# Attention shares once per block for all heads, and convolution rows as one 512-column matmul in passes two to four

## What is computed

```python
# attention, for each head h (e is es[src] + ed[dst] after a leaky ReLU)
ex    = exp(e_h - m[dst])
den   = segment_sum(ex, dst)
alpha = ex / maximum(den[dst], 1e-16)
out   = segment_sum(alpha[:, None] * z_h[src], dst)          # added to x

# convolution, used twice, with a PReLU behind each
xt  = x @ W
m   = segment_sum(xt[src], dst) * Binv[:, None]              # Binv = 1/degree, 0 without edges
out = segment_sum(m[dst], src) * Dinv[:, None] + b
```

## Time and profile before

| | us |
|---|---|
| median of 3 runs (2114.61 to 2118.65) | 2115.71 |
| the profiled execution, its own time | 2117.84 |
| the span of that execution, first to last instruction | 2115.9 |
| attention phase, first matmul to the first after it in the experts phase | 478.90 to 1005.95 |
| convolutions, first matmul to the first of the feed-forward | 1243.88 to 1918.49 |

### The profile page before, as it was taken

How to read it: one execution, slowest core, us unless ns; L and a number is a source line. 1 busy time by engine, 2 the same in 40 slices (tenths; PEclk the granted TensorE clock), 3 DMA queues, 4 the chain that set the end, 5 groups by cost and what they waited for, 6 DMA issues and landing times. The chain is left out here.

```text
span 2115.9 us, 42215 instructions
## 1 busy us (share of the span) xinstructions
PE 1749.2 (83%) x13965; PEld 1581.7 (75%) x13965; DVE 1278.1 (60%) x2275; ACT 1139.2 (54%) x1914; POOL 100.7 (5%) x124
## 2 busy tenths in 40 slices
PE   0346777728898988886999969999999999997997
PEld 0235666628888888885666659999999999995785
DVE  3767888828988889896343452222331223447897
ACT  0004777738787778784333345555666565652322
POOL 2531111100000000000000000000000000000000
PEclk9866887859999999998899989999999999997998
DMA  8221555557303030301000054444454444530102
GB/s 180 33 44 43 160 160 160 160 152 139 88 13 88 13 88 13 88 1 29 0 0 0 0 121 111 111 106 127 126 132 119 118 104 119 130 97 25 30 0 61
DMA packets 142784, 173.97 MB, mean 82 GB/s; under 512 B 27412, under 2 KB 134319, under 8 KB 142541
## 3 DMA queue, kind: packets, MB, share of 16 engines
q1 hardware_dynamic: 136858, 163.51, 30.4%
q0 software_dynamic: 5808, 8.86, 2.0%
HBM read 126.24 MB, written 46.04 MB: 81 GB/s over the span
## 5 line engine op out<-in xcount | busy, mean ns | idle before, releaser
L1453 PE MATMUL ps_sets<-arena,kinds 125*125 125x195 bf16 x5000 | 451.0, 251 | 89.8 <-DVE kinds L1382 82.2
L1453 PEld LDWEIGHTS ps_sets<-arena,kinds 125*125 125x125 bf16 x5000 | 437.7, 138 | 103.2 <-DVE kinds L1382 51.5
L2031 ACT ACTIVATE onewide<-onering 125x625 fp32r (+1 forms) x500 | 361.1, 727 | 252.9 <-PE oneps L1861 250.4
L1349 ACT ACTIVATE kinds<-ed_rows,es_mask 125x625 bf16<-125x625 f32 x500 | 366.2, 808 | 110.6 <-PE ps_sets L1453 81.1
L1861 PE MATMUL oneps<-oneparts_a,onewide 125*125 125x258 f32 x2500 | 307.5, 285 | 18.4 <-ACT onewide L2031 18.4
L1861 PEld LDWEIGHTS oneps<-oneparts_a,onewide 125*125 125x125 f32 x2500 | 303.3, 188 | 19.9 <-issue 18.7
L1861 PE MATMUL oneps<-oneparts_b,onewide 125*125 125x258 f32 x2500 | 301.8, 283 | 0.0
L1861 PEld LDWEIGHTS oneps<-oneparts_b,onewide 125*125 125x125 f32 x2500 | 300.2, 187 | 0.7
L1380 DVE TENSOR_TENSOR kinds<-kinds,cnt_block 125x2500 bf16<-125x2500 bf16 x120 | 182.4, 1520 | 72.3 <-ACT kinds L1349 63.2
L1922 DVE COPY oneraw<-oneps 125x257 f32<-125x257 f32 x100 | 35.1, 419 | 311.0 <-PE oneps L1861 311.0
L1382 DVE TENSOR_TENSOR kinds<-cnt_block,kinds 125x2500 bf16<-125x2500 bf16 x120 | 182.2, 1519 | 8.9
(11 more groups left out here) (262 smaller groups left out, 1826.9 us busy)
## 6 DMA issues: line engine op xcount, KB each, us to landing
onering<-counts SPq DMA_DIRECT2D x50, 683.6 KB
onering<-countsT SPq DMA_DIRECT2D x50, 683.6 KB
countsT<-tr SPq DMA_DIRECT2D x25, 683.6 KB
counts<-blk SPq DMA_DIRECT2D x5, 3418.0 KB
cnt_block<-counts SPq DMA_DIRECT2D x25, 546.9 KB
ed_rows<-ed_dram SPq DMA_DIRECT2D x20, 273.4 KB
onering<-counts SPq DMA_DIRECT2D x50, 79.3 KB
onering<-countsT SPq DMA_DIRECT2D x50, 79.3 KB
```

What stands on the lines that cost most here:

```text
L1349: a.activation(kinds[:, slots(m)[0] + s, 0, :], ed_b[:, h, :], ACT.Relu, scale=MASK_SCALE, bias=k.es_mask[:, t0 + s, h:h + 1]).then_inc(ma ...
L1453: last = t_.matmul(ps[0:P, BANK[h % 2][u], e * W3:(e + 1) * W3], kinds[:, slots(m)[0] + s, e, u * P:(u + 1) * P], parts[:, t, h, e, :, :]. ...
L2031: a.activation(wide[:, t % RF, :], ring[:, bass.ds((i * NS + (NS * U * n + s)) % RB, 1), w, :] .rearrange("p a d -> p (a d)"), ACT.Copy).t ...
```

## The change

In the attention, `add_parts` now adds the three parts with two tensor-tensor instructions of 325 elements, into a tile that keeps all four heads; clamp, reciprocal and scaling are made once per block for all heads (`shares`), and one instruction of 1280 elements adds the block to X (`add_to_x`). Both stand at head 0 of the next block, `batch_stats` at its head 1. The wait for X moves out of the first block.

In the convolutions the row becomes `[rest 256 | top 256 | ones 2]`. Pass 0 still makes two matmuls, one with the ones (258 columns) and one of 256. Passes 1 to 3 make one matmul of 512 columns over both parts, into both halves of a PSUM bank, and DVE adds the halves while it scales: two instructions that read PSUM, with a drain between, and the bank is free after the second. The degrees that passes 1 and 3 need are sums along the rows of the tiles of pass 0, which ACT's widening instructions accumulate (`accum_out`); `row_degrees` adds them up at the start of pass 1, behind a wait for the last widening of pass 0. The inverses of pass 0 are kept for pass 2. The first and last group of tiles of each block are taken in two turns, first destination tiles 0, 1 and 2 for all five tiles, then 3 and 4; a wide tile is released in the second turn.

```diff
-        num = sb("set_num", [P, U, D1], FP32)
-        den = sb("set_den", [P, U, 1], FP32)
+        num = sb("set_num", [P, HEADS, U, D1], FP32)
+        den = sb("set_den", [P, HEADS, U, 1], FP32)
...
-                def add_parts():
-                    v.tensor_reduce(out=num[:, :, :], in_=both[:, :, :].rearrange("p u (c d) -> p u d c", c=3), axis=AXX, op=ALU.add)
-                    v.drain()
-                    v.tensor_scalar(den[:, :, :], num[:, :, DH:D1], 1e-16, None, ALU.max)
-                    v.drain()
-                    v.reciprocal(den[:, :, :], den[:, :, :])
-                    v.drain()
-                def add_to_x(j, h):
-                    for u in range(U):
-                        x = k.X[:, bass.ds(U * j + u, 1), h * DH:(h + 1) * DH].rearrange("p a d -> p (a d)")
-                        v.scalar_tensor_tensor(out=x, in0=num[:, u, 0:DH], scalar=den[:, u, :], in1=x, op0=ALU.mult, op1=ALU.add)
+                def add_parts(h):
+                    v.tensor_tensor(out=num[:, h, :, :], in0=both[:, :, 0:D1], in1=both[:, :, D1:2 * D1], op=ALU.add)
+                    v.drain()
+                    v.tensor_tensor(out=num[:, h, :, :], in0=num[:, h, :, :], in1=both[:, :, 2 * D1:W3], op=ALU.add)
+                    v.drain()
+                def shares():
+                    v.tensor_scalar(den[:, :, :, :], num[:, :, :, DH:D1], 1e-16, None, ALU.max)
+                    v.drain()
+                    v.reciprocal(den[:, :, :, :], den[:, :, :, :])
+                    v.drain()
+                    v.tensor_tensor(out=num[:, :, :, 0:DH], in0=num[:, :, :, 0:DH], in1=den[:, :, :, :].to_broadcast([P, HEADS, U, DH]), op=ALU.mult)
+                    v.drain()
+                def add_to_x(j):
+                    x = k.X[:, bass.ds(U * j, U), :].rearrange("p u (h d) -> p h u d", h=HEADS)
+                    v.tensor_tensor(out=x, in0=x, in1=num[:, :, :, 0:DH], op=ALU.add)
                     v.drain()
                 def block_kinds(j, first):
...
-                                    add_parts()
-                                if m == 4:
-                                    if first and h == 1:
-                                        dve.wait_ge(x_in, 32)
-                                    add_to_x(*before)
-                            if m == 5 and h == 0 and not first:
-                                batch_stats(v, k.X, st, mv, k.MV, j - 1)
+                                    add_parts((h - 1) % HEADS)
+                            if not first:
+                                if m == 4 and h == 0:
+                                    shares()
+                                if m == 5 and h == 0:
+                                    add_to_x(j - 1)
+                                if m == 4 and h == 1:
+                                    batch_stats(v, k.X, st, mv, k.MV, j - 1)
                             make_kinds(j, h, m)
                 block_kinds(0, True)
+                dve.wait_ge(x_in, 32)
                 with dve.Fori(1, U) as j:
                     block_kinds(j, False)
                 add_full(U - 1, HEADS - 1, ORDER)
                 v.drain()
-                add_parts()
-                add_to_x(U - 1, HEADS - 1)
+                add_parts(HEADS - 1)
+                shares()
+                add_to_x(U - 1)
...
+        inv = sb(name + "inv", [P, 2, T], FP32)
+        degree = sb(name + "degree", [P, T], FP32)
+        row_sums = sb(name + "row_sums", [P, U, NS, U], FP32)
...
-                        for w in range(U):
-                            t = s * U + w
-                            pe.wait_ge(wide_done, TB * q + t + 1 + RB * U)
-                            for kk in range(U):
-                                if t == 0:
-                                    pe.wait_ge(c_out, U * q + kk + 1)
-                                for j, (off, size) in enumerate(PART):
-                                    last = t_.matmul(ps[0:P, kk, 0:size], wide[:, t % RF, kk * P:(kk + 1) * P], rows[:, t % T, off:off + size],
-                                                     start=(t == 0 and j == 0), stop=(t == TB - 1 and j == len(PART) - 1))
-                                if t == TB - 1 and kk < U - 1:
-                                    last.then_inc(sum_done, 1)
-                            last.then_inc(wide_used, 1)
+                        turns = [(0, 1, 2), (3, 4)] if s in (0, NS - 1) else [range(U)]
+                        for some in turns:
+                            for w in range(U):
+                                t = s * U + w
+                                if some[0] == 0:
+                                    pe.wait_ge(wide_done, TB * q + t + 1 + RB * U)
+                                for kk in some:
+                                    if t == 0:
+                                        pe.wait_ge(c_out, U * q + kk + 1)
+                                    tile = wide[:, t % RF, kk * P:(kk + 1) * P]
+                                    if n == 0:
+                                        t_.matmul(ps[0:P, kk, 0:FD], tile, rows[:, t % T, F:X2], start=(t == 0), stop=False)
+                                        last = t_.matmul(ps[0:P, kk, 0:F], tile, rows[:, t % T, 0:F], start=False, stop=(t == TB - 1))
+                                    else:
+                                        last = t_.matmul(ps[0:P, kk, :], tile, rows[:, t % T, 0:2 * F], start=(t == 0), stop=(t == TB - 1))
+                                    if t == TB - 1 and kk < U - 1:
+                                        last.then_inc(sum_done, 1)
+                                if some[-1] == U - 1:
+                                    last.then_inc(wide_used, 1)
...
+                def inverse(out, m):
+                    v.tensor_scalar(num[:, 0:m], degree[:, 0:m], 1.0, None, ALU.max)
+                    v.tensor_scalar(one[:, 0:m], degree[:, 0:m], 1.0, None, ALU.min)
+                    v.drain()
+                    v.reciprocal(num[:, 0:m], num[:, 0:m])
+                    v.drain()
+                    v.tensor_tensor(out=out, in0=num[:, 0:m], in1=one[:, 0:m], op=ALU.mult)
+                    v.drain()
+                def row_degrees():
+                    for c in range(len(counts)):
+                        for s in range(U):
+                            sums = row_sums[:, :, U * c + s, :].rearrange("p i w -> p w i")
+                            if c == 0:
+                                v.tensor_reduce(out=degree[:, U * s:U * s + U], in_=sums, axis=AXX, op=ALU.add)
+                            else:
+                                v.tensor_reduce(out=num[:, U * s:U * s + U], in_=sums, axis=AXX, op=ALU.add)
+                        v.drain()
+                    if len(counts) > 1:
+                        v.tensor_tensor(out=degree[:, :], in0=degree[:, :], in1=num[:, :], op=ALU.add)
+                        v.drain()
+                    inverse(inv[:, 1, :], T)
                 def means_out(n, i):
                     q = U * n + i
@@ -1919,23 +1959,27 @@
                             dve.wait_ge(sum_done, (U - 1) * q + kk + 1)
                         else:
                             dve.wait_ge(wide_used, TB * (q + 1) + RF)
-                        v.tensor_copy(raw[:, kk, :], ps[0:P, kk, 0:F + 1]).then_inc(c_out, 1)
-                    v.drain()
-                    v.tensor_scalar(num[:, :], raw[:, :, F], 1.0, None, ALU.max)
-                    v.tensor_scalar(one[:, :], raw[:, :, F], 1.0, None, ALU.min)
-                    v.drain()
-                    v.reciprocal(num[:, :], num[:, :])
-                    v.drain()
-                    v.tensor_tensor(out=inv[:, :], in0=num[:, :], in1=one[:, :], op=ALU.mult)
-                    v.drain()
-                    for kk in range(U):
-                        if n % 2 == 0:
-                            v.tensor_scalar(tmp[:, kk, :], raw[:, kk, 0:F], inv[:, kk:kk + 1], None, ALU.mult)
+                        hi, lo = ps[0:P, kk, F:2 * F], ps[0:P, kk, 0:F]
+                        share = inv[:, n % 2, bass.ds(i * U + kk, 1)]
+                        if n == 0:
+                            v.tensor_copy(raw[:, kk, :], ps[0:P, kk, 0:F + 1]).then_inc(c_out, 1)
+                        elif n == 2:
+                            v.tensor_scalar(raw[:, kk, 0:F], lo, share, None, ALU.mult)
+                            v.drain()
+                            v.scalar_tensor_tensor(out=tmp[:, kk, :], in0=hi, scalar=share, in1=raw[:, kk, 0:F],
+                                                   op0=ALU.mult, op1=ALU.add).then_inc(c_out, 1)
                         else:
-                            v.scalar_tensor_tensor(out=full[:, kk, :], in0=raw[:, kk, 0:F], scalar=inv[:, kk:kk + 1], in1=bias[:, n // 2, :],
-                                                   op0=ALU.mult, op1=ALU.add)
```

(25 more changed lines are left out.)

10 lines of the change are left out of this document (3 added, 7 removed).

## The result

| | before | after |
|---|---|---|
| median of the runs side by side, 4 each | 2115.16 us (2111.09 to 2118.65) | 2091.72 us (2090.25 to 2092.53) |
| profiled execution, its span | 2117.8, 2115.9 | 2091.97, 2090.3 |
| attention, first to last matmul | 504.6 | 488.7 |
| from there to the first matmul of the convolutions | 260.4 | 267.0 |
| convolutions, first to last matmul | 656.4 | 643.7 |

What follows compares the result with a forecast made beforehand. DVE was taken to set the pace in the attention, PE alone in the convolutions. Savings 42.6 + 1.0 + 1.5 + 20 = 65 us from 2117.8 give 2052.7; with the median 2.1 lower, 2050.6 us, range 2042 to 2080.

Steps and rivals of the forecast that it cites:

- I take 215.9 ns: Convolutions, passes 1 to 3: each merged 512-column matmul takes 215.9 ns, as the feed-forward's fp32 matmuls do.
- hand-over between load and stream: Convolutions, L1861: load of 108 ns and stream of 107 about equally long, neither hiding the hand-over; 12.2 ns a matmul.
- 42.6: Convolutions, passes 1 to 3: 1875 pairs go from 238.6 to 215.9 ns, saving 22.7 ns each, 42.6 us.
- Rival (b): Convolutions: time goes by columns, 235 ns at 512, saving only 6.8 us; time 2086.4 us; chance 0.11.
- nearly explain all: Convolutions at 1.2 GHz: matmuls take about 0.2 us each, where 257 columns alone would be 214 ns.
- it passes through: Attention: DVE's net saving of 21.5 us reaches the path, since DVE's head stays above PE's 21.8; 20 us taken.
- some 20: Attention, a sign to look for: DVE's busy time there down by some 20 us.
- a head goes from 24.1 to 22.1: Attention: 2.00 us of DVE saved per head takes a head from 24.1 to 22.1 us, above PE's 21.8.
- pass 0: Convolutions, pass 0: two turns give DVE ten matmuls more for banks 0 to 2, saving 5 x 0.2 = 1.0 us.
- the tail behind the sums: Behind the last convolution sum: `means_out` ends about 2.5 us after it instead of 4, saving 1.5 us.
- The degrees from ACT's accumulator: Convolutions, pass 0: ACT's accumulating instruction adds 0.1 us a tile, hidden; 34 us if it were 0.73.
- the reads of `ring`: Convolutions: reads go from 141 to about 156 GB/s, DMA share from 0.54 to 0.60, counted at nothing.

Runs made afterwards that it cites:

- loads_pairs: Kernel before, pairs kept, stationary columns cut from 125 to 64 in pass 1 and 32 in pass 2; spacing 118.9 and 118.3 ns.
- loads_512: Changed kernel, pass 2 loading 64 instead of 125 columns, pass 3 reading both operands as bf16 at 4-byte pitch; spacing 231.3 and 227.3 ns.
- before_unrolled: Kernel before with PE's loop over the attention's blocks written out; 2117.68 us against 2118.91, attention 498.3 us.
- pe_unrolled: Changed kernel with PE's loop over the attention's five blocks written out, other engines' loops kept; 2081.22 us, ratio 0.9814.
- sizes: Changed kernel with matmuls of 384 columns in pass 2 and 128 in pass 3, other sums left out; spacing 175.6 and 208 to 213 ns.

## Why the prediction was wrong

**The step that failed is "I take 215.9 ns".** It rested on two readings. The first took the feed-forward's matmul for a stream of 512 columns. It is not. The row of the list of groups in the kernel before:

```profile
L2258 PE MATMUL f_ps_o<-f_w,f_a 128*125 128x256 f32 x400 | 87.3, 379 | 0.6 <-ACT f_a L2210 0.6
```

The program has 200 such matmuls (5 blocks, 5 tiles, 8 parts of the hidden layer), the trace 400 records: a matmul of fp32 leaves two, each of 256 columns and 215.9 ns, where L1861's 5000 fp32r matmuls leave 5000. A record takes 512 column times for 256 columns; how often it reads a column, no run shows. It is no row of 512 columns of 4 bytes read at a column a clock. The second took the 12.2 ns above the column time at 257 columns for a hand-over between load and stream. `loads_pairs` and `loads_512` refute it: a quarter of the load under pairs takes 1.4 ns off, half of it under 512 columns 1.4. By the line above, 7 of the 12.2 ns belong to the columns (0.444 ns each where 2.4 GHz has 0.417) and 5.3 to the instruction. So a pair of 238.8 to 239.4 became 232.5 to 232.7: 6.4 ns x 1875 = 12 us instead of 42.6 (22.7 ns a pair). On the profiled executions 25.8 us came of 65; of the 39 missing, 31 are here, 6 in the attention and 4.7 between the phases, less some 2 us gained ahead of the attention and at the end. Rival (b) had the matmul, with 235 ns, and was given 0.11. Its row was in sight: at 1.2 GHz columns "nearly explain all", which fits a limit of 0.444 ns a column, as a column time is 0.833 ns there.

The Trainium skill (TensorE: Matmul & The Clock Gate, Back-to-back issue gap) gives 215.8 ns at 512 columns, for the gap of matmuls by themselves. The packed bf16 operands (215.8, 216.1) agree; the fp32r row at 232.6 does not, and there the measurement decides. The agreement with the feed-forward's 215.9 that the prediction names is none, since that row has 256 columns.

**The attention: right in DVE's work, wrong in "it passes through".** The durations of the forecast give 20 x (2.69 - 1.00) - 5 x 3.43 = 16.6 us less busy time, the rest of its 21.5 being gaps for drains. DVE's busy time over the phase fell from 457.83 to 442.14, by 15.7 (so the "some 20" named as a sign was too much). The path got 15.9 us, and 1.9 of them came back behind it, since the long instructions of `shares` and `add_to_x` of the last block stand behind the last head: 14.0 where the sum has 20. The step that failed is that a head goes from 24.1 to 22.1. The eleven heads without special work gave 1.4 to 1.6 us of their 2.0 (`before_unrolled` against `pe_unrolled`, where no standstill blurs them): they take 22.4 to 22.6 us, and in one of 22.5 PE is busy 21.7 and DVE 20.6. They alone are 5 to 6 us short. That PE's own pace holds them is likely by these shares, not tested. Heads 0 and 1 together gave what the sum has for them, next to nothing: at full clock and with the loop written out 27.1 + 24.1 before and 26.3 + 25.0 after. The sum also had no term for the turn of a block, where PE stands 2.5 to 3.8 us ahead of its first matmul, in both kernels, and I put the long block down to DVE's extra work alone. `pe_unrolled` shows that this standstill goes with the loop; it is a gain of its own, not the missing part of this one.

**Between the phases: a term that the sum didn't have.** That stretch grew by 6.6 us. 1.9 is the tail above; the rest falls in and around the experts, where nothing changed but the granted clock. The same window in the kernel before:

```profile
983.75:1243.88 260.13, 217.31 (x836) 139.29 (x836) 113.82 (x376) 80.21 (x159) 3.16 (x5) 0.88 0.06 15
```

0.88 before, 0.86 after: PE's busy time is 3.7 us longer for the same matmuls. In the other kernels that stretch took 261.7 to 263.9 us with the old attention and 263.0 to 266.7 with the new one, 1.9 of it tail, so most of the 4.7 us looks like where spells at the lower clock fell in these two traces. I call that likely, not shown.

**Right:** pass 0 gained 0.8 us (forecast 1.0) and the tail behind the sums 1.5 (forecast 1.5): the last sum over a bank ends at 1879.41, 2.3 us after the last matmul (forecast 2.5). Banks are freed at the size worked out, with two stalls of 0.1 us a block. The degrees from ACT's accumulator stayed hidden, at 187 ns each instead of 0.1 us; so did `row_degrees` and the reads of `ring` (142 GB/s, share 0.56).

## What to carry to other kernels

A matmul's time follows the type and pitch of what streams through it as well as its columns: before two matmuls are merged, find a row with the same bytes per column and two different widths, and take slope and intercept from it; a row of another type is not a substitute. Where work is taken off the pacing engine, and a second engine is busy nearly as long (here PE 22.2 and DVE 22.3 of 24.1 us), don't count the whole saving. Look at every head of the block by itself: an average hides the turn of the loop. And look at its granted clock before you compare two traces: one slow spell in a head was worth as much here as the edit of that head.

## What was not expected of the hardware

- A matmul with an fp32r moving operand (125 or 64 partitions) takes 5.3 + 0.444 ns a column at full clock (119.4 to 119.8 at 257, 175.6 at 384, 232.6 at 512), with bf16 at the same pitch 227.3 at 512, with packed bf16 216, and fp32r at twice the pitch nearly twice the time (453).
- A loop on PE with 1000 matmuls in its body costs 2.5 to 3.8 us of standstill at each turn, where the body written out has none; packets of the `instruction` queue come closer together there.
- A matmul of fp32 leaves two records in the trace (200 in the program, 400 records of L2258), one of fp32r a single one.
- At 128 columns of fp32r, spaced as the weight load sets it, the granted clock fell to 1.2 GHz for most of a pass (row of `sizes` above, clock 0.50), although PE was never idle in that window.
- ACT's `accum_out` is a second instruction of 187 ns, more than twice DVE's 83.
